# Hadamard products of the first attention phase as two rounded products, with the low parts made by VectorE

## The reference

```
x = x + tanh(g_xattn[0]) * attention(layernorm(x), ctx, ctx)      # 16 heads of 32, causal mask
x = x + tanh(g_ffn[0])   * ffn(layernorm(x))                      # below
x = x + tanh(g_xattn[1]) * cross attention with 4 key/value heads of 128
x = x + tanh(g_ffn[1])   * self attention with 16 heads of 32

ffn(x):  x = fwht(x * SU_ug) / 64;  up = x @ W_up.T * ..;  gate = x @ W_gate.T * ..
         x = fwht(silu(gate) * up * SU_dp) / 64;  return x @ W_down.T * ..
```

## Time and profile before

| | |
|---|---|
| median of 3 runs | 2037.15 us (2036.19 to 2037.26) |
| profiled execution | 2037.52 us |
| its span in the trace | 2035.8 us |
| TensorE busy | 1980.7 us, 97% |
| VectorE busy | 1243.6 us, 61% |
| ScalarE busy | 1163.2 us, 57% |
| GpSimd busy | 850.7 us, 42% |

### The profile page before, as it was taken

The page is one execution under the profiler, slowest core; times in us unless marked ns, Lnnn a source line. Parts: engine busy times, 40 slices in busy tenths (PEclk is TensorE's granted clock), DMA queues, the critical chain, the costliest instruction groups (busy, mean ns, idle before and its releaser), DMA issues. The chain is left out here.

```text
span 2035.8 us, 37478 instructions
## 1 busy us (share of the span) xinstructions
PE 1980.7 (97%) x13369; PEld 1647.6 (81%) x13369; DVE 1243.6 (61%) x2336; ACT 1163.2 (57%) x3064; POOL 850.7 (42%) x1010
## 2 busy tenths in 40 slices
PE   8999999999999999999989997899999999999998
PEld 6777777777778888898868886799999999878886
DVE  7767667666645543564445555666666666466665
ACT  6666666666643333353333445877777777455454
POOL 3526436445334000000004444888888888122222
PEclk9999999999999999999999998999999999999999
DMA  6426345344364210203003435333334332421001
GB/s 188 162 91 196 125 139 203 124 155 145 107 235 153 88 63 1 73 1 119 1 26 109 118 116 158 87 93 110 113 94 116 99 109 87 124 72 47 29 28 38
DMA packets 195371, 210.68 MB, mean 103 GB/s; under 512 B 60912, under 2 KB 135712, under 8 KB 194688
## 3 DMA queue, kind: packets, MB, share of 16 engines
q1 hardware_dynamic: 195200, 208.43, 32.6%
HBM read 128.43 MB, written 79.95 MB: 102 GB/s over the span
## 5 line engine op out<-in xcount | busy, mean ns | idle before, releaser
L1883 POOL TENSOR_TENSOR qd_rows<-qd_rows,c_rsum 112x375 f32<-112x375 f32 x256 | 202.5, 812 | 79.6 <-DVE c_rsum L2013 73.1
L2019 DVE TENSOR_TENSOR c_pT_lo<-c_turned,c_pT_hi 128x336 fp32r<-128x336 f32 x256 | 128.6, 503 | 123.5 <-ACT c_pT_hi L1958 123.5
L1949 ACT ACTIVATE qd_rows<-c_score,c_nmax 112x375 f32<-112x375 f32 x256 | 147.3, 575 | 87.1 <-DVE c_nmax L2008 87.1
L1314 ACT ACTIVATE b_silu<-b_gate,ab_scales 128x512 f32<-128x512 f32 (+1 forms) x64 | 40.7, 637 | 254.9 <-PE b_up L1443 254.9
L1380 DVE SCALAR_TENSOR_TENSOR b_hidden<-b_up,ab_scales,b_silu 128x512 f32<-128x512 f32 (+1 forms) x64 | 43.7, 683 | 197.5 <-ACT b_silu L1314 197.5
L2311 POOL TENSOR_TENSOR f_probs<-f_probs,f_rsum 112x448 f32<-112x448 f32 x64 | 59.8, 934 | 211.6 <-DVE f_rsum L2437 211.6
L535 ACT ACTIVATE a_probs<-a_score,a_nmax 112x375 f32<-112x375 f32 x256 | 144.8, 576 | 2.5 <-DVE a_nmax L708 2.4
L2008 DVE TENSOR_REDUCE c_nmax<-c_score 112x1 f32<-112x375 f32 x256 | 137.7, 538 | 0.5 <-PE c_score L2090 0.4
L1292 POOL TENSOR_TENSOR ab_zT<-ab_zT,keep_ln_eps 128x1 f32<-128x1 f32 x1 | 0.2, 189 | 298.7 <-DVE ab_zT L1414 298.7
L2351 ACT ACTIVATE f_probs<-f_score,f_nmax 112x112 f32<-112x112 f32 x256 | 87.3, 353 | 63.9 <-DVE f_nmax L2432 63.0
L962 PE MATMUL a_turned<-keep_ident,a_probs 112*128 112x112 f32 x768 | 122.3, 268 | 1.1 <-DVE a_pT L714 0.7
(11 more groups left out here) (354 smaller groups left out, 6111.0 us busy)
## 6 DMA issues: line engine op xcount, KB each, us to landing
q<-q_qT SPq DMA_DIRECT2D x14, 1024.0 KB, 5.7
qd_raws<-q SPq DMA_DIRECT2D x64, 224.0 KB, 3.0
v<-bq_raw SPq DMA_DIRECT2D x48, 256.0 KB, 2.1
qd_raws<-v SPq DMA_DIRECT2D x64, 192.0 KB, 2.8
k<-bq_raw SPq DMA_DIRECT2D x16, 752.0 KB, 4.0
qd_raws<-k SPq DMA_DIRECT2D x64, 188.0 KB, 2.4
wug<-a_ug_turned SPq DMA_DIRECT2D x32, 256.0 KB, 2.2
bq_raw<-in_ctx_dram SPq DMA_DIRECT2D x15, 512.0 KB
```

What stands on the lines that cost most here:

```text
L1883: pool.tensor_tensor(probs[:, n % AHEAD, 0:T], probs[:, n % AHEAD, 0:T], rsum[:, n % (2 * H):n % (2 * H) + 1].broadcast_to([S, T]), ALU.mu ...
L1949: act.activation(probs[:, n % AHEAD, 0:T], score[n % AHEAD][0:S, 0:T], ACT.Exp, bias=nmax[:, c:c + 1], accum_out=sums[:, c:c + 1]).then_in ...
L2019: dve.tensor_tensor(pT[1][:, t % 2, :, j, :], src, f32(pT[0][:, t % 2, :, j, :]), ALU.subtract).then_inc(pT_split, 1)
```

## The change

Each of the 30 Hadamard products becomes two rounded products that add up in the same bank: the matrix (whose entries are 1 and -1) by the high part of the moving operand, then by its low part. ScalarE's copy now writes the high part, rounded; a new VectorE instruction behind it subtracts it from the bank to give the low part (`down_lo`, 16 times, 128x512; `zT_lo`, 14 times, 128x448). Who used `outp` next had waited for the copy alone and now waits for the subtraction, since that reads the bank as well. The copies go to two blocks of weight buffers that are unused in this phase. ScalarE does `copy_z` ahead of `values_out` at n = 5, not behind it. The construction of the matrix takes other scratch tiles and has the same number of instructions. The wait for the store of the last rotated block moves from the copy of the turned block to the copy of the rotated one.

```diff
-        "hadamard": m.sb("hadamard", [P, P]),
+        "hadamard": m.sb("hadamard", [P, P], F32R),
...
+        second_hi, second_lo = (ab["wu"][n][:, 1, :, :, :].rearrange("p n c k -> p (n c k)") for n in range(2))
+        zT = [second_hi[:, n * DC * S:(n + 1) * DC * S] for n in range(2)]
+        downT = [second_lo[:, n * 4 * P:(n + 1) * 4 * P] for n in range(2)]
...
-                    if kind == "down" and u:
+                    if kind == "rotate" and u:
                         act.wait_ge(down_stored, 16 * u)
-                    out = down_turned[:, :]
+                    out = downT[0] if kind == "down" else down_turned[:, :]
...
-                act.activation(zT[:, :], outp[:, 0:DC * S], ACT.Copy).then_inc(z_copied, 1)
+                act.activation(zT[0], outp[:, 0:DC * S], ACT.Copy).then_inc(z_copied, 1)
...
+                    if n == 5 and b >= 2 and cur:
+                        copy_z(b - 2)
                     if n == 5 and cur:
                         values_out(b, 1)
-                    if n == 5 and b >= 2 and cur:
-                        copy_z(b - 2)
...
+            def down_lo(b, n):
+
+                number, kind, u = job(b, n)
+                if kind == "down":
+                    dve.wait_ge(job_copied, number + 1)
+                    dve.tensor_tensor(downT[1], outp[:, :], f32(downT[0]), ALU.subtract).then_inc(down_split, 1)
+
+            def zT_lo(b):
+                dve.wait_ge(z_copied, b + 1)
+                dve.tensor_tensor(zT[1], outp[:, 0:DC * S], f32(zT[0]), ALU.subtract).then_inc(z_split, 1)
...
+                    if n == 6 and cur:
+                        down_lo(b, 5)
                     if n == 6 and b >= 2 and cur:
                         rotated_lo(b - 2)
...
                         sum_keys(b, 0)
+                        down_lo(b, 1)
...
+                    if n == 5 and b >= 2 and cur:
+                        zT_lo(b - 2)
...
                     pe.wait_ge(job_copied, job(b, i)[0] + 1)
+                    if job(b, i)[1] == "down":
+                        pe.wait_ge(down_split, job(b, i)[2] + 1)
...
-                    pe.wait_ge(z_copied, b + 1)
+                    pe.wait_ge(z_split, b + 1)
...
-                    pe.matmul(outp[:, :], keep["hadamard"][:, :], down_turned[:, :], start=True, stop=True).then_inc(job_done, 1)
+                    pe.wait_ge(down_split, u + 1)
+                    pe.matmul(outp[:, :], keep["hadamard"][:, :], downT[0], start=True, stop=False)
+                    pe.matmul(outp[:, :], keep["hadamard"][:, :], downT[1], start=False, stop=True).then_inc(job_done, 1)
...
-                pe.wait_ge(z_copied, b + 1)
+                pe.wait_ge(z_split, b + 1)
...
-                pe.matmul(values[:, 0:DC * S], keep["hadamard"][:, :], zT[:, :], start=True, stop=True).then_inc(z_rotated, 1)
+                pe.matmul(values[:, 0:DC * S], keep["hadamard"][:, :], zT[0], start=True, stop=False)
+                pe.matmul(values[:, 0:DC * S], keep["hadamard"][:, :], zT[1], start=False, stop=True).then_inc(z_rotated, 1)
```

More of the change, by code:

```diff
@@ L163, in phase_a @@
     RING = 4
-    stage, xres, tmp, signs, z, zT, xr = (ab[name] for name in ("stage", "xres", "tmp", "signs", "z", "zT", "xr"))
+    stage, xres, tmp, signs, z, xr = (ab[name] for name in ("stage", "xres", "tmp", "signs", "z", "xr"))
     x_stored, k_stored, v_stored, xr_stored, xres_loaded = (ab[name] for name in ("x_stored", "k_stored", "v_stored", "xr_stored", "xres_loaded"))
@@ L240, in phase_a @@
         job_done, job_copied, lowest_set = sems("job_done", "job_copied", "lowest_set")
+        down_split, z_split = sems("down_split", "z_split")
         x1_counted, x1_moments, x1_shifted, x1_scaled, z_done, z_summed = sems(
@@ L756, in rotated_lo @@
                                          scalar=float(D) ** -0.5, in1=f32(xr[0][:, :, :]), op0=ALU.mult, op1=ALU.subtract).then_inc(xr_split, 1)
+            def down_lo(b, n):
[6 more added lines that the diff above has]
+                dve.tensor_tensor(zT[1], outp[:, 0:DC * S], f32(zT[0]), ALU.subtract).then_inc(z_split, 1)
             def hadamard(stage):
-                source, target = (had_tmp if (HADAMARD_STAGES - n) % 2 else keep["hadamard"] for n in (stage, stage + 1))
+                rough = (down_turned[:, 0:P], had_tmp[:, :])
+                source, target = rough[stage % 2], keep["hadamard"][:, :] if stage + 1 == HADAMARD_STAGES else rough[1 - stage % 2]
                 if stage:
@@ L763, in hadamard @@
                 else:
-                    source = keep["ident"]
+                    source = keep["ident"][:, :]
                     dve.wait_ge(ident_made, 1)
-                (first, second), (sums_, differences) = halves(source[:, :], 1 << stage), halves(target[:, :], 1 << stage)
+                (first, second), (sums_, differences) = halves(source, 1 << stage), halves(target, 1 << stage)
                 dve.tensor_tensor(sums_, first, second, ALU.add).then_inc(hadamard_made, 1)
@@ L1470, in rotate_late @@
                 pe.wait_ge(z_copied, 1)
-                pe.matmul(up[LATE % 2][:, 0:DC * S], keep["hadamard"][:, :], zT[:, :], start=True, stop=True).then_inc(z_rotated, 1)
+                pe.matmul(up[LATE % 2][:, 0:DC * S], f32(keep["hadamard"][:, :]), zT[:, :], start=True, stop=True).then_inc(z_rotated, 1)
             for c in range(DC):
@@ L1478, in _ @@
             pe.wait_ge(early_copied, 1)
-            pe.matmul(y[2][:, 0:DC * S], keep["hadamard"][:, :], zT[:, :], start=True, stop=True).then_inc(early_rotated, 1)
+            pe.matmul(y[2][:, 0:DC * S], f32(keep["hadamard"][:, :]), zT[:, :], start=True, stop=True).then_inc(early_rotated, 1)
             for t in range(1, STEPS):
```

## The result

The changed kernel takes 2045.66 us in the median of 6 runs (2042.14 to 2048.93), the kernel before 2037.2 (2036.19 to 2040.19): a ratio of 1.0042, 95% interval 1.0032 to 1.0052. It is slower by 8.5 us. The forecast was 2043 and the range 2037 to 2050. The profiled execution took 2047.45 us; its page begins as follows (against the earlier trace rows).

The account below looks back on a forecast made before the run. TensorE was taken to bound the first phase: waits of 13.4 and 1.8 us, less 11.3 saved, give +3.9; a 1.7 us clock fall makes +5.6, so 2043 us, range 2037 to 2050.

Parts of the forecast that it names:

- the step that decides: Batches with down jobs, n = 6: `weigh(b, 2)` waits for a subtraction queued behind the next batch's maximum; TensorE idles 1.81 us.
- TensorE bounds the phase, so every part adds up: First phase: TensorE busy 299.5 of 300 us, so every 0.1 us saved or waited there changes the time.
- The rival that hidden waits behind the place would absorb the new ones: Wait at n = 6 mostly absorbed by hidden TensorE waits: 2026 if all vanished, 2034 with half; chance 0.12.
- Rotate jobs at n = 3: Eight jobs ahead of the scores: 0.95 us becomes 0.56, saving 0.39 each, together 3.1 us.
- At n = 7: Eight rotate jobs: product and two rounded ones behind it, 1.33 us, become 1.02; 0.31 each, together 2.5 us.
- rotate_z, 0.41: Fourteen z rotations: 0.86 us becomes 0.45 for two rounded products of 448 columns; 0.41 saved each, together 5.7 us.
- The bound from two products of 512 columns: Lower bound for rotate_z: at the price of two 512-column products (0.51 us), it saves 0.35 us each.
- down_lo at n = 1: Eight subtractions between key sums and statistics on VectorE: hidden, cost 0, at most 0.1 us each.
- zT_lo costs 0.13 us: Subtraction at n = 5 makes job 5 start late: 0.13 us for 14 batches, 1.8 us; bounds 0 and 2.8.
- down_lo at n = 6: `weigh(b, 2)` waits for this subtraction: 1.81 us in seven batches, 0.7 in batch 15; together 13.4, bounds 11.5 and 14.5.
- The clock, one fall in seven: Behind the seven new 1.81 us waits, one fall to 1.2 GHz for 3.4 us, costing 1.7 us; bounds 0 and 12.
- the case without a fall: Rival: the wait at n = 6 is there but the clock holds; +3.9 us, 2041.2; chance 0.29.

## Why the prediction was right, point by point

The answer in short: the step that decides, the wait of `weigh` behind the maximum, held in its cause, its places and its length. The sizes of the terms were less good than their sum. Without the clock +3.9 us were forecast, and the profile less its falls has +4.1, but that is in part luck: the waits were put 0.8 us too high (15.2 for 14.4), the saving as much (11.3 for 10.5 in the stretch), and the two errors cancel.

*TensorE bounds the phase, so every part adds up.* Shown: the waits alone cost 14.4 us, the products alone save 10.5, and the two with the falls give the whole. The rival that hidden waits behind the place would absorb the new ones has fallen.

*Rotate jobs at n = 3, 0.39 us each.* TensorE's timeline of the changed kernel has the pair ahead of the scores in batch 6 at

```profile
244.26 0.39 PE L1025 MATMUL a_outp<-ab_wu_lo,keep_hadamard 128*128 128x512 f32 x1
244.49 0.40 PE L1026 MATMUL a_outp<-ab_wu_lo,keep_hadamard 128*128 128x512 f32 x1
244.81 0.43 PE L933 MATMUL a_score<-a_kT_hi,a_qT_hi 32*112 32x376 f32 x4
```

that is 0.55 us for 0.95: 0.40. *At n = 7, 0.31:* 1.01 for 1.33, and the start of the pair lies another 0.07 us nearer to the transposes ahead of it (0.22 us behind them where it was 0.29), which the step had not counted: 0.38. *rotate_z, 0.41:* 0.35; the estimate from a group of four took all of the pair at the price of matmuls inside a group. The first of the pair takes 0.31 us and the second 0.20 (batch 10 above), so a pair alone costs more than two places inside a group of four. The bound from two products of 512 columns was the right value. The sum by these is 11.1 us where 11.3 was forecast and 10.5 measured in the stretch. The difference is accounted for: the stretch begins behind the first of the rotate jobs (0.4), and the wait ahead of the second phase is 0.3 longer. By the four passes that "FP8 and Floating Point Precision" in the Trainium skill (TensorE Precision Notes) gives to true fp32, halved, the estimate was 12.9; the trace does not reach that, with 0.51 us left of 0.86 and 0.55 of 0.95.

*down_lo at n = 1 is hidden.* No wait for it appears on TensorE in any profile.

*zT_lo costs 0.13 us.* It costs 0.06 in the batches with ug jobs: the first transpose of job 5 starts only 0.01 us later, but the second and later ones 0.07, and `weigh` 0.06 later. In the batches with down jobs this is in the 1.85. The idle time of some 0.1 us that was to show ahead of job 5 is not there.

*down_lo at n = 6 costs 1.81 us, seven times, and 0.7 once.* 1.85 with the part of zT_lo (forecast: 1.94), and 0.72. Together with zT_lo the forecast was 15.2 us, the measured sum 14.4 (the kernel with the waits alone). The subtraction began at the end of the reduction as worked out, and TensorE needed 0.14 us from its end. That its place in the queue makes the wait is shown by the kernel in which it alone was moved.

*The clock, one fall in seven, 1.7 us.* That waits of this length bring falls was right, their number was too small. The profile has two, other profiles with the same wait two and three, each at 1.5 to 1.7 us. The median moved by 8.5 us where the sum without falls is 3.9 to 4.1, so an ordinary run has about 4.5 us more. If that is the clock, it is about three falls by the price of one. The granted clocks of the timed runs agree roughly: their median is 0.9875 for the changed kernel and 0.99 for the kernel before beside the experiments, and the runs at 0.991 and 0.985 are the fastest and the slowest (2042.14 and 2048.93 us). But these are clocks of whole executions. The kernel before has runs from 0.986 (2041.95 us) to 0.991 too, so the later phases contribute, and how many falls lie in the first phase in runs without a profile is not known. This is the term by which the forecast of 2043 most likely fell short of 2045.66.

Its premise was weak: that the wait of 2.16 us "left the clock at full" was seen in one execution, and in six of the nine later profiles the same wait was followed by 6.8 us at half clock. So it was no evidence for the case without a fall. Right ahead of it are products of 512 columns, while the new waits lie between transposes and small products; whether that makes a difference was not tried.

## What to carry to other kernels

An instruction that another engine waits for belongs in its queue at the point where its input is ready, ahead of anything that waits for later work: here one subtraction behind a maximum that waited for the next batch's scores cost more than thirty cheaper products gained. When one engine is dense, put a gain and a new wait on the same ledger, start to start, and look for work that the waiting engine could do first; two moves in VectorE's queue and one in TensorE's turned a loss of 8.5 us into a gain of 11. And price a new idle gap of TensorE at its length plus the risk that the clock falls behind it, and read that risk from more than one execution.

## What the runs showed of the hardware

- The clock falls to 1.2 GHz for 3.4 us behind short idle gaps of TensorE, and not each time: in the first phase behind 7 of 7 gaps of 2.32 us, 7 of 21 of 1.72 us and none of 14 of 0.36 or 0.37 us, all between transposes and small matmuls in a phase that is otherwise dense. Each of these falls costs 1.5 to 1.7 us. A gap of 2.16 us behind products of 512 columns was followed by 6.8 us at 1.2 GHz in 6 of 10 executions.
- A full fp32 product of 448 columns takes 0.86 us of TensorE's queue from start to start, two rounded ones 0.51 us; of 512 columns ahead of the scores, 0.95 and 0.55. Less than half is saved; the first of two rounded products takes 0.31 us and the second 0.20.
- Where job 5 of kind ug became free just as TensorE came to it, `weigh` started 0.05 to 0.06 us later (1.72 to 1.73 us behind it); with the subtraction 0.4 us earlier it was 1.67 again.
